# A decoder layer: the feed-forward's inner layers kept turned, their norms applied one layer late

## The reference, cut to what matters

```python
amp = sigmoid(x @ amp_w + amp_b)
ph = tanh(x @ ph_w + ph_b) * pi
h = (cos(ph) + sin(ph)) * amp
for l in range(2):
    e = h @ ent_w[l] + ent_b[l]                 # 512 -> 2048
    h = _layer_norm(h + e @ ent_pw[l] + ent_pb[l], ln3_g[l], ln3_b[l])
    t = einsum('bsd,pdf->pbsf', h, path_w[l]) + path_b[l][:, None, None, :]
    mod = cos(phase[l]) + sin(phase[l])
    h = _layer_norm(h + sum(t * mod[:, None, None, :], axis=0), ln4_g[l], ln4_b[l])
x = _layernorm(x + h)
```

## Time and profile before

| | |
|---|---|
| median of 3 runs | 908.15 us (905.5 to 908.82) |
| profiled execution | 906.72 us |
| its span | 904.8 us |
| PE busy | 861.6 us (95%), 5812 matmuls |
| DVE busy | 677.2 us (75%) |
| ACT busy | 548.4 us (61%) |
| POOL busy | 487.0 us (54%) |
| TensorE clock granted, mean | 0.989 of full |

### The profile page before, as it was taken

How to read it: one execution, slowest core, us unless ns; L and a number is a source line. 1 busy time by engine, 2 the same in 40 slices (tenths; PEclk the granted TensorE clock), 3 DMA queues, 4 the chain that set the end, 5 groups by cost and what they waited for, 6 DMA issues and landing times.

```text
span 904.8 us, 19451 instructions
## 1 busy us (share of the span) xinstructions
PE 861.6 (95%) x5812; PEld 717.6 (79%) x5812; DVE 677.2 (75%) x2060; ACT 548.4 (61%) x1666; POOL 487.0 (54%) x796
## 2 busy tenths in 40 slices
PE   6899999999899999999999999998999999999993
PEld 6778888888787888888888887776778778878773
DVE  5778888888878878777787866758884675666556
ACT  6756556666666757575656655755736645664563
POOL 3465655465856646454655521337751781593387
PEclk9999999999999999999999999999999999999997
DMA  6655353543584846575584548434002002001001
GB/s 204 228 167 174 118 166 124 174 162 129 179 265 141 255 129 211 158 233 153 160 236 137 179 125 272 169 109 148 1 24 71 0 12 82 1 1 47 1 0 47
DMA packets 79475, 117.49 MB, mean 130 GB/s; under 512 B 8480, under 2 KB 42272, under 8 KB 78752
## 3 DMA queue, kind: packets, MB, share of 16 engines
q1 hardware_dynamic: 75792, 112.81, 40.1%
q10 hardware_dynamic: 3600, 3.68, 1.3%
HBM read 58.25 MB, written 17.31 MB: 84 GB/s over the span
## 4 chain that ended last, share of the span: by engine, by line
PE 59%; DVE 6%; POOL 2%; SPq 2%; issue 2%; ACT 2%; DMA 1%; POOLq 0%; DVEq 0%; ACTq 0%
PE bank L161 45%; PE bank L1513 4%; PE bank L2040 3%; PE bank L1536 2%; PE bank L1499 2%; PE bank L1540 1%; SPq L702 1%; DVE stats L1942 1%; DVE w_ffn L1727 1%; ACT prob L1106 1%; POOL hT L1835 1%; DMA xres<-in_x 1%; PE bank L1449 1%; DVE y L1956 1%; DVE bank L1257 0%
## 5 line engine op out<-in xcount | busy, mean ns | idle before, releaser
L1106 ACT ACTIVATE prob<-bank,nmax 128x128 f32<-128x128 f32 (+1 forms) x512 | 209.6, 432 | 25.8 <-DVE nmax L1257 23.3
L161 PE MATMUL bank<-w_ffn,hT 128*128 128x512 f32 x768 | 188.5, 396 | 1.1 <-DVE w_ffn L1727 0.9
L1257 DVE CUSTOM_DVE_ANT_0 bank<-bank,mask 128x128 f32<-128x128 f32 (+1 forms) x512 | 168.2, 386 | 3.4 <-DVE cv L1202 2.3
L161 PEld LDWEIGHTS bank<-w_ffn,hT 128*128 128x128 f32 x768 | 140.2, 188 | 29.9 <-POOL hT L1835 1.4
L919 POOL TENSOR_TENSOR zone<-raw,zone 128x256 fp32r<-128x256 f32 x128 | 96.3, 785 | 59.8 <-ACT zone L1053 59.8
L1513 PE MATMUL bank<-ident,prob 128*128 128x128 f32 x768 | 119.4, 278 | 0.8 <-ACT probT L1119 0.4
L1119 ACT ACTIVATE probT<-bank 128x512 f32<-128x512 f32 x97 | 58.5, 604 | 96.3 <-PE bank L1540 96.1
L1106 ACT ACTIVATION_READ_ACCUMULATOR prob<-bank,nmax 128x1 f32 x512 | 110.9, 217 | 0.0
L161 PE MATMUL bank<-xT,w_q 128*128 128x256 f32 x768 | 102.5, 286 | 3.0 <-DVE o L1278 3.0
L161 PEld LDWEIGHTS bank<-xT,w_q 128*128 128x128 f32 x768 | 98.9, 193 | 8.0 <-issue 3.1
L1896 ACT ACTIVATE ht<-bank,cols 128x128 f32<-128x128 f32 x192 | 72.4, 459 | 53.2 <-PE bank L2040 53.2
(11 more groups left out here) (133 smaller groups left out, 1510.4 us busy)
## 6 DMA issues: line engine op xcount, KB each, us to landing
q<-stage SPq DMA_DIRECT2D x192, 128.0 KB, 2.8
k<-kstage SPq DMA_DIRECT2D x48, 256.0 KB, 4.0
x<-xres SPq DMA_DIRECT2D x16, 512.0 KB, 4.6
raw<-in_ent_wT SPq DMA_DIRECT2D x32, 256.0 KB, 4.1
raw<-in_ent_pw SPq DMA_DIRECT2D x32, 256.0 KB, 4.4
raw<-in_path_w SPq DMA_DIRECT2D x8, 512.0 KB, 3.9
xres<-in_x SPq DMA_DIRECT2D x8, 512.0 KB, 4.0
x1b<-x SPq DMA_DIRECT2D x8, 512.0 KB, 5.1
```

The costliest lines, as they stand in the source:

```text
L161: ins = t.matmul(out, lhs(a, k), rhs(b, k), start=first and n == 0 and m == 0, stop=last and n == len(kts) - 1 and m == 2, skip_group_chec ...
L1106: ins = s.activation(prob[:, u, c * width:(c + 1) * width], banks[u][:, c * width:(c + 1) * width], ACT.Exp, scale=-1.0, bias=nmax[:, i % ...
L1257: ins = v.tensor_tensor_reduce(scored, scored, mask[:, S - width:S], scale=-1.0, scalar=3e38, op0=ALU.add, op1=ALU.min, accum_out=nmax[:, ...
```

## The change

The first three layers keep the features on partitions. Weights are now the stationary operand and `hT`, 512 tokens wide, the moving one, so a layer's result is already turned and feeds the next without a transpose.

A norm's mean is taken out of the weights: each row of a matrix has its mean over the output features removed (`means` on ACT, `centre` on DVE), so a layer's output has mean zero over the features. The norm's gain goes into the next layer's rows, its shift into a column of constants `c` for each layer (`bias_partials` on POOL and DVE, `column_sum`/`column_total` as products with ones, `column_centred` on DVE).

1/std: ACT squares the layer's output (`square`), POOL and DVE add the four feature tiles, PE multiplies by a matrix of ones, which puts each token's sum on all partitions, ACT takes a reciprocal root, DVE refines it by a Newton step (`inverse_of`). It is applied when the next layer's result leaves PSUM (`turned_out`), one layer late, since a factor by token goes through a product. The constant column is scaled the same way by standing ahead of it. For the last layer, which has tokens on partitions as before, four one-column products of squares with ones give the second moments, POOL the power (`rstd2`), and `unit` applies it by row.

In `flush`: `means(0)` on ACT at the end of the last cross turn, `means(1)`, `means(2)` between the gates, `stage_hi`/`stage_lo` of stages 0 and 1 before `wout`'s `add_and_measure` on DVE, stage 2 and 3 at the start of `ffn_phase`; stage 1's load goes to the last cross turn, stage 2's and 3's into `flush`. The `eb` products go. Block 0's load and transposes of the second input move behind the second moments. Tables are switched twice a block on ACT.

SP, ACT and DVE in the last cross turn and in `flush`, and the row means:

```diff
+                        pr.wait_full(q, t, ("cv", TT - 1))
+                        q.sem_inc(s_passed, 1)
+                        ffn.load_stage(q, 1)
...
                     if t is last_cross and i == NG - 1:
                         s.preload_act_table_set("silu_and_others")
+                        ffn.means(s, 0)
                     if t is flush and i == 0:
...
                         gate(0)
+                        ffn.stage_hi(s, 0)
                         gate(1)
+                        ffn.means(s, 1)
                     if t is flush and i == 1:
                         gate(2)
-                        ffn.stage_hi(s, 0)
+                        ffn.stage_hi(s, 1)
+                        ffn.means(s, 2)
                         gate(3)
...
                     if t is flush and i == 1:
+                        ffn.stage_lo(v, 0)
                         gate(1)
+                        ffn.centre(v, 1)
                         gate(2)
+                        ffn.stage_lo(v, 1)
...
                         ffn.half_columns(v)
+                        ffn.centre(v, 0)
                         gate(0)
                     if t is flush and i == 1:
-                        ffn.stage_lo(v, 0)
+                        ffn.bias_partials_of_second(v)
+                        ffn.centre(v, 2)
                         gate(3)
...
+    def means(self, s, n):
+        s.wait_ge(self.s_wraw[n], 32)
+        for c in range(KT):
...
+            if at:
+                s.wait_ge(self.s_mean, self.mean_of(n, c) - 1)
+            s.activation(self.root[:, :], self.stage_raw[n][:, c, :], ACT.Copy, scale=1.0 / D,
+                         accum_out=self.row_mean[:, at:at + 1]).then_inc(self.s_mean, 1)
```

`ffn_phase` on ACT:

```diff
-            ffn.stage_hi(s, 1)
+            ffn.stage_hi(s, 2)
+            ffn.stage_hi(s, 3)
...
+                for s_ in range(TURNED - 1):
+                    hi(s_, 0)
+                    for j in range(KT):
+                        square(s_, j)
+                    for j in range(1, KT):
+                        hi(s_, j)
+                    s.wait_ge(s_zv, step_of(VECTOR_STEPS, b, s_, "total"))
+                    s.activation(sum_hi[:, :], squares[0], ACT.Copy).then_inc(s_za, 1)
+                    k.wait_full(("s", s_))
+                    s.activation(root[:, :], banks[plan.bank(("s", s_))][:, :], ACT.Abs_reciprocal_sqrt, bias=ffn.eps, scale=1.0 / D).then_inc(s_za, 1)
```

`ffn_phase` on DVE:

```diff
-            ffn.stage_lo(v, 1)
+            ffn.stage_lo(v, 2)
...
+                if b == 0:
+                    stored(v)
+                    column_sum(0)
+                    column_centred(0)
+                    v.tensor_copy(ffn.ones_r[:, :], ffn.ones[:, :])
+                    ffn.stage_lo(v, 3)
...
+                for s_ in range(TURNED - 1):
+                    for j in range(KT):
+                        turned_out(s_, j)
+                    lo(s_, 0)
+                    sum_of_squares(s_)
+                    lo(s_, 1)
...
+                    lo(s_, 2)
+                    lo(s_, 3)
...
+                    inverse_of(s_)
```

`ffn_phase` on PE, in the layers turned and in block 0:

```diff
+                    if s_ > 0 and c < KT - 1:
+                        for n in range(KT):
+                            if c == 0:
+                                k.wait_free((f"z{s_}", n))
+                            products(n, ((0, 0), (1, 0)))
+                        t.wait_ge(s_zv, step_of(VECTOR_STEPS, b, s_ - 1, f"lo{c}"))
+                        for n in range(KT):
+                            products(n, ((0, 1),))
+                        return
...
+                def column_total(s_):
+                    t.wait_ge(ffn.s_col, ffn.column(s_, "sum"))
+                    k.wait_free(("a", s_))
+                    k.filled(("a", s_), t.matmul(banks[plan.bank(("a", s_))][:, 0:KT], ffn.ones[:, :], ffn.c[:, s_, :], start=True, stop=True))
...
+                for c in range(KT):
+                    turned_pass(0, c)
+                    if b == 0 and c == 0:
+                        column_sum(0)
+                    if b == 0 and c == 1:
+                        column_total(0)
```

More of the change, by code:

```diff
@@ L1587, in gate_products, with step_of, ffn_order @@
                           lambda h, c: xT[:, :, h, c, :], range(KT))
[L1590 to L1601, removed]
+def gate_products(t, bank, gates, xT, gate, m):
+    off = {"amp": OFF_AMP, "ph": OFF_PH}[gate]
+    return split_products(t, bank[:, :].rearrange("p (a s) -> p a s", a=2), lambda h, c: gates[:, h, off + c * D + m * P:off + c * D + (m + 1) * P],
+                          lambda h, c: xT[:, :, h, c, :], range(KT))
+LAYERS = 2 * NL
+TURNED = LAYERS - 1
+_SCALAR = ("hi0", "sq0", "sq1", "sq2", "sq3", "hi1", "hi2", "hi3", "sum", "root", "square")
+_VECTOR = ("z0", "z1", "z2", "z3", "lo0", "pair", "total", "lo1", "rest", "lo2", "lo3", "newton", "inverse")
+SCALAR_STEPS = (_SCALAR, _SCALAR, ("hi0", "sq0", "hi1", "hi2", "hi3", "sq1", "sq2", "sq3"))
+VECTOR_STEPS = (_VECTOR, _VECTOR, ("z0", "z1", "z2", "z3", "lo0", "lo1", "lo2", "lo3", "pair", "total", "mean"))
+POOL_STEPS = (("pair",), ("pair",), ("pair", "rstd"))
+def step_of(steps, b, s, name):
+    return b * sum(map(len, steps)) + sum(map(len, steps[:s])) + steps[s].index(name) + 1
+def ffn_order(b):
+    first, last = b == 0, b == NB - 1
+    turned = [("xt", i) for i in range(BT)]
+    order = [("z0", n) for n in range(KT)]
+    order += [("c", 0), ("a", 0)] if first else [] if last else turned
+    order += [("z1", n) for n in range(KT)]
+    order += [("c", 1), ("s", 0), ("a", 1), ("c", 2)] if first else [("s", 0)]
+    order += [("z2", n) for n in range(KT)]
+    order += [("a", 2), ("s", 1), ("c", 3)] if first else [("s", 1)]
+    order += [("mm", 0), ("mm", 1), ("m", 0)] + (turned if first else []) + [("mm", 2), ("mm", 3)]
     return order + ([] if last else [(w, m) for m in range(KT) for w in ("ph", "amp")])
@@ new lines, in body @@
+                if 0 < b and not last:
+                    for i in range(BT):
+                        x2T_hi(k, i)
+                for s_ in range(TURNED - 1):
[8 more added lines that the diff above has]
+                    s.activation(root[:, :], banks[plan.bank(("s", s_))][:, :], ACT.Abs_reciprocal_sqrt, bias=ffn.eps, scale=1.0 / D).then_inc(s_za, 1)
+                    s.wait_ge(s_za, step_of(SCALAR_STEPS, b, s_, "root"))
+                    s.activation(newton, root[:, :], ACT.Square).then_inc(s_za, 1)
@@ L1910, in body @@
+                if not last:
+                    s.preload_act_table_set("silu_and_others")
+                hi(TURNED - 1, 0)
+                square(TURNED - 1, 0)
+                for j in range(1, KT):
+                    hi(TURNED - 1, j)
+                for j in range(1, KT):
+                    square(TURNED - 1, j)
+                if b == 0:
+                    for i in range(BT):
+                        x2T_hi(k, i)
                 if not last:
@@ L1988, in finish @@
                     v.wait_ge(s_sum, n)
[L1989 to L1998 removed]
+                    statistics(BT + i)
@@ new lines, in second_moments, with second_input @@
+                def second_moments():
+                    t.wait_ge(s_zv, step_of(VECTOR_STEPS, b, TURNED - 1, "total"))
+                    k.wait_free(("m", 0))
+                    bank = banks[plan.bank(("m", 0))]
+                    for i in range(BT):
+                        ins = t.matmul(bank[:, i:i + 1], squares[0][:, i * P:(i + 1) * P], ffn.ones[:, 0:1], start=i == 0, stop=i == BT - 1, skip_group_check=True)
+                    k.filled(("m", 0), ins)
+                def second_input():
+                    t.wait_ge(s_xb[(b + 1) % 2], 16 * ((b + 1) // 2 + (b + 1) % 2))
+                    for i in range(BT):
+                        x2T(k, i, b + 1)
@@ L2070, in tensor @@
+                if not last:
+                    for i in range(BT):
+                        k.wait_drained(("xt", i))
+                    for m in range(KT):
+                        gate(k, "ph", m)
+                        gate(k, "amp", m)
             every_block(t, body)
```

548 lines of the change are left out of this document (345 added, 203 removed).

## The result

The changed kernel takes 929.4 us (median of 4 runs, 926.8 to 930.8) beside 907.8 us for the kernel before (905.5 to 908.8): a ratio of 1.0238, 95% interval 1.0208 to 1.0268. The forecast was 913 with a range of 902 to 924: the sign was right, the size wrong by 16 us. The profiled execution has a span of 927.8 us where before it was 904.8, 23.0 more.

The account below looks back on a forecast made before the run. PE's own work was taken to bound the middle blocks, DVE the end. Block 1 starting 11.7 us later, less 5.6 in two middle blocks, plus 0 in the last, gave +6.1: 912.8 or 914.2, stated as 913, range 902 to 924.

Parts of the forecast that it names:

- Start of block 0: End of the attention: added ACT and DVE preparation makes block 0 start at 615 to 616 instead of 612.29.
- PE's idle behind the means: Near 585 us: means(0) on ACT delays a copy that PE waits for, leaving PE idle 2.6 us.
- The wait in `column_total(0)`: Block 0, after PE's second pass: PE waits 8.5 us for DVE's column_sum(0), restarting at about 631.
- The clock's fall behind it: Block 0, after the column_total(0) wait: lowered granted clock costs PE 1.7 us of work.
- PE's own work: Each block: layer products 0.230 us each, 44.2 in all; sums of squares add 0.9, second moments 0.8.
- the upper bound of the moments: Four fp32 one-column second-moment products: 3.0 us at most, twice two ones products read as about 1.5; 0.8 taken.
- Waits between layers: Layer boundaries of each block: PE waits 1.4 us in sum, 1.8 with DVE slightly stretched by POOL; ends 0.7 and 3.5.
- Last block: Block 3 to the end: stays at 65.0 us (63.5 to 67), no gain, as the end hangs on DVE.
- The tail behind PE's last product: End of the last block: 17 us after PE's last product instead of 13.7.
- the second: Rival at layer boundaries: POOL stretches DVE's operations, waits 3.5 a block, block 1 starts at 706; +14.8, 923; chance 0.2.
- The first: Rival in block 0: DVE reaches column_sum(0) in time, PE's wait is below 4 us; -4.1, 904; chance 0.25.
- The third: Rival in the middle blocks: DVE's four units and gate steps keep the block at 74.8; +11.7, 919; chance 0.1.

Follow-up runs that it names:

- e2: Changed kernel with GpSimd's residual additions of a block's first two boundaries held until lo3 and its pair of squares made on DVE: 915.2 us, ratio 1.0110.
- e10: e9 with the next input's transposes back in their old pass and block 0's last layer doing low-weight products last: 908.8 us, ratio 1.0018.
- e3: Changed kernel with ACT's means of stage 0 placed behind the two copies that PE waits for: 928.1 us, ratio 1.0250.
- e1: Changed kernel with GpSimd's four residual additions at each block's first two boundaries waiting for lo3, DVE's last operation there: 923.2 us, ratio 1.0182.
- e4: Changed kernel with DVE's gate 3 and column_sum(0) ahead of stage 2's bias sum and centring, low parts of stages 2 and 3 later: 923.8 us, ratio 1.0209.
- e6: e5 with the order of e4 (column_sum(0) ahead of stage 2's bias sum and centring, low parts later): 914.3 us, ratio 1.0074.
- e9: e6 plus e3's edit, DVE's low parts of stages 2 and 3 cut and moved, middle blocks' input transposes one pass later: 910.2 us, ratio 1.0040.
- e5: e2 with GpSimd's stage 3 bias sum moved behind block 0's first boundary and that block's residual additions behind the second: 913.8 us, ratio 1.0073.

## Why the prediction was wrong

Length of each part in the profiled executions, us (the first block's forecast is 701.8 less 615.5):

| | before | forecast | changed | e2 | e10 |
|---|---|---|---|---|---|
| block 0 | 77.8 | 86.3 | 91.1 | 89.4 | 83.5 |
| block 1 | 74.9 | 72.1 | 77.4 | 72.8 | 73.0 |
| block 2 | 74.7 | 72.1 | 75.1 | 72.8 | 72.8 |
| block 3 to the end | 65.0 | 65.0 | 68.3 | 65.2 | 65.5 |

- **Start of block 0: right.** 615 to 616 forecast, 615.93 measured; PE's idle behind the means 2.6 and 2.81. That this idle is a loss by itself was only partly so (e3).
- **The wait in `column_total(0)`: right.** 8.5 forecast, restart near 631; 9.41, restart 632.0. The clock's fall behind it was put at 1.7; the 32 products behind it took 9.03 us, 1.6 more than the 7.4 of such a run later. The stretch by GpSimd was counted here, by the 1.03 of the earlier trace rows, and it came.
- **PE's own work: right for the new products** (second moments 0.92 for 0.8, sums of squares 0.24 a product; the upper bound of the moments was read too high, as the two ones products took 1.31 us, 603.89 to 605.20, and not 1.5). The layers' products were a little low: taking the other parts off e2's 71.2 us of PE work leaves (71.2 - 22.4 - 1.7 - 0.9 - 0.9) / 192 = 0.236 where I put 0.230, 1.1 us a block. That difference includes short stops that the timeline does not name.
- **Waits between layers: the step that failed.** I gave DVE's operations at a boundary 0.69 each and 0.4 us in all for GpSimd's company. The 0.69 came from reading a bank; the operations of a boundary read two SBUF tensors, as those at 1.03 did. With GpSimd silent they too take 0.69 (e2), but with a stream of 1.29 + 4 x 1.15 us beside them 1.1 to 1.3. The third block's named stops were 3.1 us, not 1.8, and the same stretch sits in block 0 and the last block. e2 takes it away: 1.7, 4.6, 2.3 and 3.0 us in the four blocks, 11.6 in all, which is also what the ratios differ by (0.0128 of 907). Of the 16.4 us between forecast and result this is 11.6.
- **What went with it: the half clock behind the second moments**, 1.6 us each in the second and the last block, which I had not thought of, since I expected PE to wait only 0.4 there. It is inside the 11.6.
- **Last block: the length right but for the same stretch, and partly by luck.** The third unit came 53.9 us into the block, not 50.9; with the boundaries quiet (e2) it came at 50.95 and the block is 65.2. But two terms behind that 50.9 were wrong and cancel. The first half of the last layer is 24 products, 5.5 us at my own 0.23, and I put 7.4; it took 6.18, in e2 5.84. From the first unit to the third I put 5.7; it took 6.95 (906.51 to 913.46), of which 1.0 is one more operation of two SBUF tensors beside GpSimd, 1.74 us (910.87) where its like took 0.75. That PE's saving does not reach the end held. The tail behind PE's last product was 15.6 us, not 17, because PE itself ran at the half clock.
- **The rest**, about 5 us, is block 0 beyond its forecast in e2 (3.1, of which the wait is 0.9 and a longer clock fall 1.3) and 0.7 in each middle block.

**Of the rivals**, the second was the case: its block 1 start (706, measured 707.0) and its waits (3.5 a block) fit; its total of 923 took 2.2 us off for the two middle blocks, which together got 2.8 longer (1.6 of this is the clock's fall, about 2 the layers' products), and gave the last block 1 us where it lost 3.3. The first needed a wait under 4. The third (whose sum, 908.15 + 11.7, is 919.9 and not 919) has the right figure for the third block (74.8, measured 75.1) by another mechanism: e2 leaves the units and gate steps as they are and its blocks take 72.8. The 0.2 that I gave the second was too little: the row that priced it stood among mine.

"SBUF — State Buffer", section "SBUF: two separate sides", of the Trainium skill says that GpSimd and a DVE operation with two SBUF inputs take their shared port pair in turn, each for a whole instruction. By that rule a DVE operation of 0.69 and a residual piece of 0.70 (e1) would, as an estimate, come round every 1.39 us. The rows above have 1.22 and 1.15, so as measured they overlap a little, but the rule would have put the boundary on the right side of my 0.69.

Not tried: a version that gives DVE's part of the preparation to another engine, so that what DVE must do in block 0 shrinks; whether the change then gains stays open.

## What to carry to other kernels

Price an operation by a row with the same kinds of operands and the same neighbours, not by one of the same length: here a bank read at 0.69 stood in for a two-tensor read beside GpSimd, at 1.1 to 1.3, and five such operations at a boundary undid a saving of 2 us a block. A helper engine that takes an addition off the critical engine can cost it more than the addition: moving 0.69 us of work back to DVE made every boundary shorter. A wait that is moved can come back at another place of the same stage (e4, e6, e9), so a change of order is judged by the length of the stage, and not by the stop that went.

## What the runs showed of the hardware

- Beside GpSimd's stream DVE's `TENSOR_SCALAR` with a single SBUF tensor in is stretched as well: the centrings took 0.48 each in e5 (1.91 / 4) and 1.03 in e4 (4.11 / 4). Operations that read a bank were not: four drains of `z` beside GpSimd's bias sum took 3.19 us in e6 (644.45), and 3.21 in the changed kernel with GpSimd idle (653.40), 0.80 each.
- The clock's fall does not go by the length of the stop. Behind 9.41 us of idle 32 products took 9.03 us (changed kernel) or 10.41 (e2), behind 5.69 us 10.33 (e5); and 0.59 to 0.60 us with the second moments brought the half clock in two of the four blocks of the changed kernel, in one of four in e1 and in none of four in e4.
- A product of one column in full fp32 is recorded as two, and four of them hold PE for 0.92 us (753.95 to 754.87).
